# A fused attention kernel: TensorE's other work moved ahead of the scores at a head's switch, and spread over the heads

## The reference

```python
x = L0_attn_x                                   # (16, 512, 128), 16 heads of 8
x = x + 0.5 * ffn(layernorm(x))
x = x + attention(layernorm(x))
x = x + 0.5 * ffn(layernorm(x))

def ffn(x):       # rows and weight are rounded to a 6-bit grid, 32 elements to a scale
    return dequant(quant6(x)) @ dequant(quant6(w)).T + bias

def attention(x):
    Q, K, V = (split_heads(x @ W + b) for W, b in ((Wq, bq), (Wk, bk), (Wv, bv)))
    s = Q @ K.T / sqrt(8) + 0.3 * log(mask + 1e-6)[None]   # mask: (16, 512, 512), one per head
    return merge(softmax(s) @ V) @ Wo + bo
```

## Time and profile before

| | |
|---|---|
| median of three runs | 915.6 us (914.88 to 918.88) |
| profiled execution, its own time | 913.18 us |
| its span, first to last instruction | 911.2 us |
| PE busy | 734.2 us (81%), 4355 matmuls |
| ACT busy | 671.4 us (74%) |
| DVE busy | 529.4 us (58%) |
| POOL busy | 187.2 us (21%) |
| mean granted clock of PE | 0.942 |

### The profile page before, as it was taken

How to read it: one execution, slowest core, us unless ns; L and a number is a source line. 1 busy time by engine, 2 the same in 40 slices (tenths; PEclk the granted TensorE clock), 3 DMA queues, 4 the chain that set the end, 5 groups by cost and what they waited for, 6 DMA issues and landing times.

```text
span 911.2 us, 12886 instructions
## 1 busy us (share of the span) xinstructions
PE 734.2 (81%) x4355; PEld 259.3 (28%) x4355; DVE 529.4 (58%) x1308; ACT 671.4 (74%) x795; POOL 187.2 (21%) x164
## 2 busy tenths in 40 slices
PE   0367617889889888999989889999889888998944
PEld 0043301232222222333223224333233112322334
DVE  8776566464544376756874676567943323465264
ACT  1488726778878888888877788887768878888811
POOL 0306642003333120033251020123630000020011
PEclk9987757899999999999999999999999999999986
DMA  5539549973777775536776655377666555555201
GB/s 145 124 115 369 186 120 351 268 207 110 208 225 223 191 204 159 162 117 182 225 220 215 186 176 166 115 206 210 194 183 221 174 162 164 177 172 156 75 1 50
DMA packets 56068, 162.10 MB, mean 178 GB/s; under 512 B 14120, under 2 KB 24496, under 8 KB 45578
## 3 DMA queue, kind: packets, MB, share of 16 engines
q1 hardware_dynamic: 51740, 154.36, 55.6%
q0 software_dynamic: 1808, 5.94, 2.1%
q10 hardware_dynamic: 2446, 0.89, 0.5%
HBM read 117.87 MB, written 43.29 MB: 177 GB/s over the span
## 4 chain that ended last, share of the span: by engine, by line
PE 50%; DVE 16%; DMA 11%; ACT 9%; issue 9%; SPq 3%; POOL 1%; ACTq 0%; DVEq 0%; POOLq 0%
PE S_PS L1523 20%; PE O_PS L1537 17%; DVE S_PS L1159 8%; ACT BIG L693 8%; DMA BIG<-shift_rows 6%; PE R_PS L1546 3%; PE F_PS L1428 3%; PE F_PS L1423 2%; DMA PART<-trig_parts 2%; PE P_PS L1428 1%; DMA k_parts<-PART 1%; SPq L331 1%; SPq L334 1%; PE P_PS L1461 1%; PE S_PS L1703 1%
## 5 line engine op out<-in xcount | busy, mean ns | idle before, releaser
L693 ACT ACTIVATE BIG<-S_PS 128x1024 f32<-128x1024 f32 x512 | 508.6, 1023 | 148.5 <-PE S_PS L1523 143.9
L1523 PE MATMUL S_PS<-BIG 98*128 98x512 bf16 x1024 | 305.1, 391 | 77.5 <-DVE S_PS L1159 45.8
L1537 PE MATMUL O_PS<-BIG,VX 128*9 128x512 f32 x2048 | 271.3, 603 | 0.9 <-issue 0.9
L1159 DVE COPY S_PS<-BIG 128x1024 f32<-128x1024 f32 x128 | 152.0, 1223 | 150.9 <-ACT BIG L693 149.4
L1523 PEld LDWEIGHTS S_PS<-BIG 98*128 98x128 bf16 x1024 | 74.8, 98 | 341.3 <-ACT BIG L693 129.2
L1172 DVE RECIPROCAL RD<-R_PS 128x16 f32<-128x16 f32 x64 | 16.4, 257 | 128.8 <-PE R_PS L1546 128.3
L544 POOL TENSOR_TENSOR XDT<-PART 128x512 bf16<-128x512 f32 x24 | 26.5, 1104 | 258.9 <-ACT PART L661 258.9
L1537 PEld LDWEIGHTS O_PS<-BIG,VX 128*9 128x9 f32 x2048 | 30.9, 88 | 112.8 <-issue 98.3
L521 POOL TENSOR_TENSOR BIG<-BIG,BFH 128x512 f32<-128x512 f32 x16 | 21.9, 1400 | 187.0 <-DVE BIG L991 134.4
L521 POOL TENSOR_TENSOR X<-X,BFH 128x512 f32<-128x512 f32 x16 | 26.0, 1652 | 151.0 <-DVE BIG L991 76.0
L553 POOL TENSOR_TENSOR PART<-PART 128x512 f32<-128x512 f32 x32 | 37.1, 1158 | 69.3 <-DVE PART L1062 68.9
(11 more groups left out here) (190 smaller groups left out, 744.1 us busy)
## 6 DMA issues: line engine op xcount, KB each, us to landing
BIG<-ln_masks SPq DMA_DIRECT2D x62, 1024.0 KB, 6.6
ln_masks<-BIG SPq DMA_DIRECT2D x16, 1024.0 KB, 7.7
BIG<-q_parts SPq DMA_DIRECT2D x63, 192.0 KB
BIG<-k_parts SPq DMA_DIRECT2D x63, 144.0 KB
BIG<-q_parts SPq DMA_DIRECT2D x63, 128.0 KB
q_parts<-PART SPq DMA_DIRECT2D x9, 768.0 KB, 3.8
k_parts<-PART SPq DMA_DIRECT2D x18, 384.0 KB, 4.4
BIG<-k_parts SPq DMA_DIRECT2D x63, 96.0 KB
```

The lines of the kernel that those rows point to most:

```text
L693: act.activation(E[:, m % 2, j, 2 * pair:2 * pair + 2, :], S_PS[:, pair, :, :], ACT.Exp, scale=LOG_WEIGHT)\
L1159: ve.tensor_copy(S_PS[:, pair, :, :], LNM[:, slot, 2 * pair:2 * pair + 2, :]).then_inc(s["seeded"], 1)
L1523: mm = pe.matmul(S_PS[:, pair, i, :], KT[0:ALL_ROWS, slot, K_COL[j], 128 * kb:128 * kb + 128], QT[0:ALL_ROWS, slot, j, :], start=False, st ...
L1537: mm = pe.matmul(O_PS[32 * j:32 * j + HD + 1, :], VX[:, slot_of(n), j, kb, h, :], E[:, m % 2, j, kb, :], start=kb == 0, stop=kb == T - 1)
```

## The change

- TensorE: the other work of ticks 0 and 1 stands ahead of the scores, and turn_o stands in tick 1, ahead of s1, instead of behind s4.
- VectorE: o_norm in tick 1; other work stands ahead of the seeding copies of its tick; the attention statistics are a step of their own (`stats2`).
- The tables are new, and differ by group. The first layers of groups 2 and 3 run two groups ahead (`LATE`, in q = 0 and q = 1), their rounding in two halves, with `F_PS` and `XDT[1]` for all batches. The chains start at ticks (3, 27, 51, 75) in q = 1 and 2. `LAST` starts at tick 10.
- GpSimd's order and SP's places for its stores follow the tables. SP stores the masks 9 to 12 before the second head's stack is loaded, and mask 8 after the first stack has landed.

```diff
-FIRST = dict(stats_ve=(0, 2, 4, 8), centre_ve=9, lnexp_act=10, rstd_ve=12, reduce_ve=16, scales_ve=18,
-             to_grid_ve=20, from_grid_ve=24, turn_pe=(28, 30, 36, 38), xd_copy_act=(29, 31, 37, 39),
-             ffn_pe=(32, 34, 40, 42), add_ve=(33, 36, 41, 44), lnexp1_act=(39, 48), rstd1_ve=(40, 49),
-CHAIN = (48, 64, 80, 96)
-SECOND = dict(turn_pe=0, xnt_act=1, q_pe=4, q_act=5, k_pe=8, k_act=9, v_pe=12, v_ve=13, hi_q_ve=8, mid_q_ve=10,
-              hi_k_ve=11, mid_k_ve=13, norms_k_pe=14, k_top_ve=16, norms_q_pe=18, sq_ve=19, sqrt_act=21,
-              row_ve=24, turn_bound_pe=26, bound_act=27)
-LAST = dict(turn_pe=(50, 58, 66, 74), at_act=(51, 59, 67, 75), out_pe=(54, 62, 70, 78), add_ve=(57, 65, 73, 81),
-            centre_ve=83, lnexp_act=84, rstd_ve=88, reduce_ve=89, scales_ve=92, to_grid_ve=96, from_grid_ve=99,
-            turn_xd_pe=(104, 110, 116, 122), xd_copy_act=(105, 111, 117, 123), ffn_pe=(108, 114, 120, 126),
+FIRST = dict(stats_ve=(0, 2, 4, 8), centre_ve=9, lnexp_act=10, rstd_ve=12, reduce_ve=14, scales_ve=16,
+             to_grid_ve=17, from_grid_ve=19, turn_pe=(22, 24, 28, 32), xd_copy_act=(22, 24, 28, 32),
+             ffn_pe=(24, 27, 31, 35), add_ve=(25, 28, 32, 36), stats1_ve=(27, 29, 33, 37), lnexp1_act=(31, 39),
+LATE = ((dict(stats_ve=(50, 52), lnexp_act=54, rstd_ve=60, centre_ve=64, reduce_ve=66, scales_ve=68, to_grid_ve=72,
+              from_grid_ve=74, turn_pe=(82, 90), xd_copy_act=(82, 90), ffn_pe=(84, 92), add_ve=(85, 93),
+              stats1_ve=(88, 96), lnexp1_act=98, rstd1_ve=99),
+         dict(stats_ve=(82, 83), lnexp_act=87, rstd_ve=91, centre_ve=97, reduce_ve=98, scales_ve=101, to_grid_ve=104,
+              from_grid_ve=106, turn_pe=(110, 118), xd_copy_act=(110, 118), ffn_pe=(112, 120), add_ve=(113, 121),
...
+        (dict(stats_ve=(26, 28), lnexp_act=30, rstd_ve=32, centre_ve=33, reduce_ve=34, scales_ve=36, to_grid_ve=41,
+              from_grid_ve=44, turn_pe=(50, 58), xd_copy_act=(50, 58), ffn_pe=(52, 60), add_ve=(53, 61),
...
+              from_grid_ve=98, turn_pe=(110, 118), xd_copy_act=(110, 118), ffn_pe=(112, 120), add_ve=(113, 121),
+CHAINS = ((43, 59, 75, 91), (3, 27, 51, 75), (3, 27, 51, 75), ())
+APART = dict(norm_ve=-2, turn_pe=0, xnt_act=1, q_pe=5, q_act=5, hi_q_ve=6, mid_q_ve=9, k_pe=13, k_act=13, hi_k_ve=14,
+             mid_k_ve=18, norms_k_pe=17, k_top_ve=17, norms_q_pe=19, sq_ve=19, sqrt_act=20, v_pe=21, v_ve=22,
+             row_ve=23, turn_bound_pe=25, bound_act=26)
+CLOSE = APART | dict(k_pe=9, k_act=9, hi_k_ve=10, mid_k_ve=14, v_pe=13, v_ve=14)
+SECOND = (CLOSE, APART, APART, {})
+AMID = dict(turn_pe=(10, 18, 26, 34), at_act=(10, 18, 26, 34), out_pe=(12, 20, 28, 36), add_ve=(13, 21, 29, 37),
+            stats_ve=(16, 24, 32, 40), lnexp_act=42, centre_ve=49, rstd_ve=50, reduce_ve=56, scales_ve=58,
+            to_grid_ve=64, from_grid_ve=72, turn_xd_pe=(75, 82, 90, 98), xd_copy_act=(75, 82, 90, 98),
+            ffn_pe=(77, 84, 92, 100), add_ffn_ve=(77, 85, 93, 101))
+ALONE = dict(turn_pe=(14, 22, 30, 38), at_act=(14, 22, 30, 38), out_pe=(16, 24, 32, 40), add_ve=(17, 25, 33, 41),
...
+             to_grid_ve=56, from_grid_ve=58, turn_xd_pe=(62, 70, 78, 86), xd_copy_act=(62, 70, 78, 86),
+             ffn_pe=(64, 72, 80, 88), add_ffn_ve=(65, 73, 81, 89))
+LAST = ({}, AMID, AMID, ALONE)
...
         def first_bank(n, j):
-            return (P_PS, F_PS)[j % 2]
+            return F_PS if n in (2, 3) else (P_PS, F_PS)[j % 2]
...
             lnm_stored(sp, 3)
             load_x(1)
             store_mask(0)
-            store_mask(8)
+            for h in range(9, 13):
+                store_mask(h)
             load_stack(sp, 1)
             load_shift(sp, 1)
             sp.wait_ge(s["first_stack"], K_LOADS)
-            for h in range(9, 13):
-                store_mask(h)
+            store_mask(8)
...
             def attention(q):                      # VectorE
                 for tick in range(TICKS):
+                    if k == 1 and m >= 2:
+                        o_norm(m - 2)
+                    background(q, tick)
                     if k >= STEPS - 2 and m + 1 < NQ * NH:
                         seed(m + 1, k - STEPS + 2)
-                    if k == 5 and m >= 2:
-                        o_norm(m - 2)
...
             def attention(q):                      # TensorE
                 for tick in range(TICKS):
-                    if k == 0:
+                    if k < 2:
                         background(q, tick)
+                    if k == 1 and m >= 2:
...
+                        pe.wait_ge(s["bound_sq"], 3 * (1 + QB * q + done))
+                        pe.wait_ge(s["bound_copied"], 1 + QB * q + turned)
+                        turn_o(m - 2)
                     scores(m, k)
                     if k % 2 and m >= 1:
                         weighted(m - 1, k // 2)
-                    if k == 4 and m >= 2:
...
-                        turn_o(m - 2)
-                    if k:
+                    if k >= 2:
                         background(q, tick)
```

More of the change, by code:

```diff
@@ L265, in calls_of @@
         def calls_of(n, k):
-            return 2 if k == 1 or (k == 2 and n == NQ - 1) else 1
+            halved = {0: range(2, NQ), 1: range(2 * NQ), 2: range(NQ - 1, NQ)}
+            return 2 if n in halved[k] else 1
         def calls_before(n, k):
@@ L602, in _, with batch @@
             pool.memset(VX[:, 1, :, :, :, HD:HD + 1], 1.0).then_inc(s["vx_ones"], 1)
-            for q in range(NQ):
-                after, before = q < NQ - 1, q > 0
-                if after:
-                    bias_before(q + 1)
-                    for j in range(QB):
-                        chain(q + 1, j)
-                        start_after(q + 1, j)
-                        if j == 2 and before:
-                            bias_after(q - 1)
-                elif before:
-                    bias_after(q - 1)
+            def batch(n, j):
+                chain(n, j)
+                start_after(n, j)
+            bias_before(1)
+            batch(1, 0)
+            batch(1, 1)
+            bias_before(2, range(0, 2))
+            batch(1, 2)
+            batch(1, 3)
+            bias_before(2, range(2, 4))
+            batch(2, 0)
+            batch(2, 1)
+            bias_before(3, range(0, 2))
+            bias_after(0)
+            batch(2, 2)
+            batch(2, 3)
+            bias_before(3, range(2, 4))
+            batch(3, 0)
+            batch(3, 1)
+            bias_after(1)
+            batch(3, 2)
+            batch(3, 3)
+            bias_after(2)
             bias_after(NQ - 1)
@@ L741, in attention @@
             def attention(q):
-                before, after = q > 0, q < NQ - 1
                 for tick in range(TICKS):
@@ L1612, in background @@
[L1612 to L1621 removed]
+                normed = max(m - 2 + (k > 1), 0)
@@ new lines, in background @@
+                if q == 0:
+                    if tick in FIRST["turn_pe"]:
+                        turn_xd0(1, FIRST["turn_pe"].index(tick))
+                    if tick in FIRST["ffn_pe"]:
+                        ffn0(1, FIRST["ffn_pe"].index(tick))
+                for j, c in enumerate(CHAINS[q]):
+                    n = q + 1
+                    if tick == c + SECOND[q]["turn_pe"]:
+                        turn_xn(n, j)
+                    if tick == c + SECOND[q]["q_pe"]:
+                        project_q(n, j)
+                    if tick == c + SECOND[q]["k_pe"]:
+                        project_k(n, j)
+                    if tick == c + SECOND[q]["v_pe"]:
+                        project_v(n, j)
+                    if tick == c + SECOND[q]["norms_k_pe"]:
+                        norms_k(n, j, normed)
+                    if tick == c + SECOND[q]["norms_q_pe"]:
+                        norms_q(n, j)
+                    if tick == c + SECOND[q]["turn_bound_pe"]:
+                        turn_bound(n, j, normed)
```

332 lines of the change are left out of this document (183 added, 149 removed).

## The result

| | before | after |
|---|---|---|
| median | 915.8 us (914.88 to 918.88) | 884.15 us (882.32 to 885.29) |
| profiled execution | 913.18 us | 884.51 us |
| its span | 911.2 us | 882.6 us |
| mean granted clock of PE | 0.942 | 0.943 |

The medians here are of four executions. The ratio is 0.9647, with a 95% interval of 0.9619 to 0.9675; the forecast was 883 us. In a second comparison, on another chip than the first eight experiments, the changed kernel took 883.56 us, the kernel before 911.78 (ratio 0.9688, 0.9654 to 0.9722).

The account below looks back on a forecast made before the run. TensorE was taken as the bound after a DMA-bound start. Terms -21.3 - 8.3 + 0.2 - 2 + 3 - 4 = -32.4 us took 913.2 to 880.8, plus 2.4 for the median: 883 us; sum's own range 871 to 898, overall 866 to 903.

Parts of the forecast that it names:

- A: turn_o moves from tick 4 to tick 1, into TensorE's wait before the second score pair: 21.3 us gained.
- D: VectorE's background ahead of seeding copies, first-layer rounding halved and earlier: late seeds cost 3 us, not 5; 2 us gained.
- F: At the start, masks 9 to 12 stored before the second head's stack: 4 us gained, between 3 lost and 10 gained.
- Rival 1: At the head's switch, turn_o's loads and the product before the first scores don't fit: 893 to 904 us; chance 0.14.
- B: TensorE's other steps move to tick 0, with less at ticks 1 to 5 and 6 to 7: 8.3 us gained.
- C: At the head's switch, late work plus tick 0 work overflows TensorE's idle time: 6.6 us for 6.4, nothing gained.
- e7: ScalarE's exponential of tick 7, the last in a head; steps at ticks 6 or 7 were said to delay only it.
- e0: ScalarE's exponential of tick 0, the first in a head; 9.96 us from one to the next in a light head.
- e6: ScalarE's exponential of tick 6 in a head; its 0.45 us idle wait before was forecast to fall to about 0.2.
- rival 3: VectorE's seeding copies come late behind its background; decides from 0.52 us a head, some 921 to 946 us; chance 0.06.
- E: ScalarE's 24 copies of q and k now stand between a head's first two exponentials: 3 us lost.
- Rival 2: TensorE's half-clock drops end once both holes at the switch are filled: 868 us with the start's upper bound; chance 0.16.

## Why the prediction was right, point by point

The time is right, 883 for 884.15, and so is its largest term. Two others missed by about 10 us each with opposite signs, and that they nearly cancel is luck. Between the two profiled executions, from which the sum was made, the gain is 28.7 us for its 32.4; the medians are 31.65 apart. (The sum's own range ended at 898; its bounds A 12, D 2 and F 7 add up to 904.)

*A, turn_o: right.* 9.77 us a light head for the forecast 9.75, s1 0.07 us behind its seed there, no overflow from turn_o's weight loads, and 22 us lost when it goes behind s1. In ten of the 61 switches from the third head's on s1 comes 0.13 to 0.68 us behind the second seed, which the forecast had called a sign of being wrong; that is 3 us in all. What the term missed is its condition. Alone, on the old tables, it gave its size in the last group but little in all, since the bound's steps then move and more stacks come late. Rival 1 (the switch does not hold the work) did not come.

*B and C, the places: right in size.* The second and third groups came at 178.0 and 174.9, forecast 174 to 178. The overflow is 0.28 us in each of seven heads of the last group (10.05 for 9.77), forecast 0.30. Moving the out-product back to tick 6 changed nothing that can be told, as the prices of B and C have it together. What B did not price is that the nine late stacks ended with the new tables, 11.3 us of TensorE's waits, and 9.7 us by what those switches take from e7 to the next e0 beyond the ordinary 1.12. The forecast had them only as "a part" of 5 us in D. Which change of the tables did it, no run shows.

*D, VectorE: wrong.* The sum expected late seeds to cost 3 us where there had been 5. By the timelines, seeds that start 0.3 us or more after e6 were late by 2.4 us in all before (two heads) and by 13.0 after (ten). That is their cost too: at these ten switches ScalarE passes 23.6 us between e7 and the next e0, where ten ordinary ones take 11.2. Six of the large ones, 6.5 us, stand behind bound_sq at tick 6; three, 6.1 us, behind rounding (1.71, 1.99 and 2.39).

The step that failed is the price of VectorE's small operations. The forecast took bound_sq at its 0.65 us, without its wait for norms_q, and took the rest as harmless; and it put GpSimd's order at nothing. Beside GpSimd's instructions such an operation takes about 1 us more: L1158 in four of the six behind bound_sq, rstd ahead of the seeds that are 1.71 and 2.39 late, two block scales (1.15 and 1.07 for 0.19 and 0.18) ahead of the one at 1.99. By an estimate from these rows, which takes the excess off each of the seven seeds, 9.7 of the 13.0 us are theirs. Only for the last, 2.39 us, does a run show it. So rival 3's mechanism was there, at 13 / 63 = 0.2 us a head, below the 0.52 at which it would have decided. The term should have been about +10, not -2; the late stacks, -10 to -11, covered it.

*E, ScalarE's copies:* no run parts them from the rest of the loaded heads, so the 3 us stay open.

*F, the start: right for the kernel before, wrong for the changed one.* On the kernel before, the masks alone gave 3.5 us for the forecast 4. In the changed one they gave nothing that can be told. The forecast named both parts that ate it, the first head 0 to 3 us later (2.3 by the store) and the next wait on the chain, which is the late seed of the third head, but took 4 us all the same. The 3 us wait of the second head is gone as said; the third head's e0, forecast 5 us earlier, came at 162.0 for 162.5.

*Rival 2, the clock: its drops went, its gain did not come.* In the heads from the fourth on, the granted clock of the kernel before is at half in three places of 3.4 us, 10.2 us in all, each just behind an ordinary switch's wait of 1.06 us. In the changed kernel none stands at such a switch, nor in any of its ten profiled variants and reruns, though its light heads still wait 1.06 us before s0. But it has two others, 10.2 us again, the longer one here, in windows of the last group:

```profile
743.90:750.70 6.80, 5.39 (x19) 1.79 (x20) 6.74 (x8) 2.05 (x2) 0.00 (x0) 0.50 0.56 198
```

It begins as TensorE waits for the latest seed, its longest wait of 3.4 us; the shorter one begins at 289.9, behind a wait of 1.9 us for another late seed. With rstd later the 3.4 us wait is gone and so is the drop, and both return in the rerun of the changed kernel. In the kernel with rstd ahead of the centring two new drops stand at the waits for bound_row. So every drop in these heads of the changed kernel and its variants lies at or behind a wait of 1.5 us or more, though not every such wait has one. The runs fit rival 2, that a filled hole ends the drops at the switches, but no run shows it by itself, and D's late seeds brought others. The Trainium skill, "TensorE: Matmul & The Clock Gate", section "What's actually happening", has the slow clock as the idle state; these drops, each at or behind a wait, agree.

The last group came at 162.3 us, forecast some 160: its seventh and eighth heads, with the late seed and the drop, are 24.6 us, with rstd later 21.4, and that group was then 159.0.

## What to carry to other kernels

Where an engine with an in-order queue waits twice at a switch, work put into the shorter hole can be free to its last tenth of a microsecond, but price what that step drags with it: here the new place alone, on the old tables, gave 0.5 to 6 us of its 21. A step put ahead of the critical work makes whatever it waits for critical too, as bound_sq, bound_row and o_copy each were here. A small operation ahead of critical work is priced by what runs beside it, not by its length alone. A sum that comes out right can hold two large errors; look at the waits by releaser, not only at the total.

## What was not expected of the hardware

VectorE's small operations on SBUF take five to seven times as long beside GpSimd's adds of 128x512 f32. Two-input ones of 128x16 take 0.86 to 1.21 us for 0.17, one of 128x1 takes 0.98, and a one-input tensor_scalar of 128x64 takes 1.16 for 0.20. One add takes 1.24 us, about the length of such a delay. Nor is it smallness that matters: in the changed kernel a rounding step of 128x2048 (L1079) that starts 1.07 us before a bias add ends takes 3.22 us for 2.29. A cast of 128x512 (L1114) takes 1.38 us for 0.42 when it starts behind a GpSimd instruction, and 0.43 when it starts 0.04 us ahead of one. So the delay is about what is left of the GpSimd instruction already running. A reduction of 2.28 us, a reciprocal (0.26), the seeding copies into PSUM (1.23), and a product of 128x128 that reads PSUM (0.29), were not slowed. It is the neighbour that does it: the same three operations took 0.17 us each ahead of the adds, and the third took 0.18 once they had ended. The Trainium skill, "SBUF — State Buffer", section "🔬 SBUF: two separate sides", tells of a port pair that VectorE and GpSimd share under a lock held for a whole instruction. These rows agree with it for two inputs. For one input it names only certain performance modes; whether the tensor_scalar and the cast ran in one, no run shows.
